# Gate features restacked by transfers, and four steps moved, in the first attention of a two-layer gated cross-attention kernel

## What is computed

```python
# queries x (layer norm), keys and values ctx; 16 batches, 128 tokens, H = 16 heads of 64
delta_x = log(clip(abs((cx - cx.T) / w), 0.001))      # delta_y alike; delta_w = log(w / w.T), delta_h alike
mul = (100.0 * stack[delta_x, delta_y, delta_w, delta_h])[..., None] * [1, 1000 ** -0.5]
emb = concatenate([sin(mul), cos(mul)])                # 16 gate features of a query-key pair
g = relu(einsum('bnmd,hd->bhnm', emb, Wg) + bg)        # one gate per head and pair
a = q @ k.T / sqrt(64)
mn = softmax(log(clip(g, 1e-6)) + a)                   # = clip(g) * exp(a), normed
x = x + tanh(g_xattn[0]) * ((mn @ v) @ Wo.T + bo)
```

## Time and profile before

| | us |
|---|---|
| median of 3 runs | 1169.16 |
| lowest and highest | 1166.68, 1172.12 |
| the profiled execution, its own time | 1164.61 |
| its span, first to last instruction | 1162.8 |

### The profile page before, as it was taken

The page is one execution under the profiler, slowest core; times in us unless marked ns, Lnnn a source line. Parts: engine busy times, 40 slices in busy tenths (PEclk is TensorE's granted clock), DMA queues, the critical chain, the costliest instruction groups (busy, mean ns, idle before and its releaser), DMA issues.

```text
span 1162.8 us, 32870 instructions
## 1 busy us (share of the span) xinstructions
PE 955.3 (82%) x12178; PEld 779.8 (67%) x12178; DVE 836.2 (72%) x1947; ACT 689.7 (59%) x1338; POOL 718.9 (62%) x811
## 2 busy tenths in 40 slices
PE   0448988899999996387878559995599999999996
PEld 0336766667777764364554248873599999999995
DVE  3997888877887775657776779985566666666663
ACT  2456878888888884145425548884354545454542
POOL 2988778886677752115341539984566766666663
PEclk9888999999999997669999869995799999999998
DMA  9276667678776756330001000000555215841251
GB/s 277 72 192 142 122 129 146 150 167 183 140 149 154 154 105 148 98 130 1 1 14 41 19 2 16 26 21 19 201 142 140 32 32 140 246 142 32 32 144 16
DMA packets 52118, 119.65 MB, mean 103 GB/s; under 512 B 7617, under 2 KB 30145, under 8 KB 51633
## 3 DMA queue, kind: packets, MB, share of 16 engines
q0 software_dynamic: 14144, 35.48, 21.3%
q1 hardware_dynamic: 35520, 80.71, 20.7%
q10 hardware_dynamic: 2352, 2.10, 0.6%
HBM read 212.54 MB, written 37.85 MB: 215 GB/s over the span
## 4 chain that ended last, share of the span: by engine, by line
PE 51%; DVE 18%; POOL 14%; ACT 6%; issue 5%; DMA 4%; POOLq 0%; ACTq 0%; SPq 0%; DVEq 0%
PE bank L2107 17%; PE bank L2121 9%; POOL PT L560 6%; PE bank L1786 6%; PE bank L1689 3%; PE bank L1766 2%; DVE nmx L1177 2%; ACT EX L1393 2%; PE bank L1728 2%; DVE h L1063 2%; PE bank L1937 2%; PE bank L1721 1%; DVE PT L923 1%; PE bank L1780 1%; DMA gates<-in_g_ffn 1%
## 5 line engine op out<-in xcount | busy, mean ns | idle before, releaser
L1623 ACT ACTIVATE yg<-bank,bms 128x128 f32<-128x128 f32 x312 | 107.8, 364 | 106.8 <-PE bank L2107 98.9
L1296 DVE TENSOR_TENSOR hm<-hf,hm 128x256 f16<-128x256 f32 x156 | 70.3, 450 | 81.5 <-ACT hm L1630 81.5
L1291 DVE SCALAR_TENSOR_TENSOR hf<-bank,bms,yg 128x128 f32<-128x128 f32 x312 | 98.1, 345 | 33.2 <-ACT yg L1623 32.0
L2107 PE MATMUL bank<-xT,wm_even 128*128 128x128 f16 x1920 | 115.6, 221 | 1.0 <-DVE xT L1303 1.0
L2107 PEld LDWEIGHTS bank<-xT,wm_even 128*128 128x128 f16 x1920 | 111.5, 99 | 2.1 <-DVE xT L1303 1.4
L560 POOL TENSOR_TENSOR PT<-PT 128x512 f16<-128x512 f32 x64 | 72.7, 1183 | 61.4 <-ACT PT L1419 61.4
L707 POOL DMA_INDIRECT out_x<-ys,sidx x39 | 62.8, 1611 | 76.2 <-DVE ys L1310 76.2
L2107 PE MATMUL bank<-xT,wm_odd 128*128 128x128 f16 x1824 | 108.0, 219 | 1.8 <-DMA wm_odd<-expert_weights 1.8
L2107 PEld LDWEIGHTS bank<-xT,wm_odd 128*128 128x128 f16 x1824 | 104.2, 98 | 2.4 <-issue 1.9
L1630 ACT ACTIVATE hm<-hf 128x256 f16<-128x256 f32 x156 | 64.5, 414 | 63.1 <-DVE hf L1291 61.7
L619 POOL TENSOR_TENSOR h<-h 128x512 f16<-128x512 f32 x32 | 40.6, 1281 | 83.0 <-DVE h L1063 81.0
(11 more groups left out here) (308 smaller groups left out, 2646.7 us busy)
## 6 DMA issues: line engine op xcount, KB each, us to landing
wm_even<-expert_weights SPq DMA_DIRECT2D x60, 1024.0 KB
wm_odd<-expert_weights SPq DMA_DIRECT2D x57, 1024.0 KB
expert_weights<-in_wcat POOLq DMA_DIRECT2D x16, 768.0 KB, 7.8
wsp<-expert_weights SPq DMA_DIRECT2D x16, 768.0 KB, 4.4
wsp<-in_wcat POOLq DMA_DIRECT2D x16, 768.0 KB, 10.3
expert_weights<-wsp SPq DMA_DIRECT2D x16, 768.0 KB, 3.3
Lst<-gate_tables SPq DMA_DIRECT2D x48, 68.0 KB, 6.0
gate_tables<-Lw SPq DMA_DIRECT2D x6, 512.0 KB, 3.3
```

The costliest lines, as they stand in the source:

```text
L1291: v.scalar_tensor_tensor(hf[:, (c // 2) % 2, c % 2, :], bank[c % 4][:, MT:2 * MT], bms[:, par, FC + c:FC + c + 1], yg[:, c % 4, :], ALU.ad ...
L1296: v.tensor_tensor(hm16[:, par, 1, c - 1:c + 1, :], hf[:, q % 2, :, :], hm16[:, par, 0, c - 1:c + 1, :], ALU.subtract).then_inc(m_hl, 1)
L1623: s.activation(yg[:, c % 4, :], bank[c % 4][:, 0:MT], ACT.Gelu, bias=bms[:, par, c:c + 1]).then_inc(m_g, 1)
L2107: ins = t.matmul(bank[c % 4][:, w * MT:(w + 1) * MT], wm16[par][:, wp, col:col + P], xT16[:, par, xp * KD + kk, :], start=(n == 0), stop=( ...
```

## The change

- **Features stacked.** The 128 feature partitions are ordered in four groups of 32 (each of 4 queries). SyncE copies them into a new tile `Fst`: for each group the high half twice and the low half once, 96 partitions. That is twelve transfers of 64 KB per batch (`stack_high`, eight; `stack_low`, four). The weight shrinks to 96 x 64, its middle 32 rows being the low half, and a query group takes four matmuls of 64 columns in place of three of 256. F16s has one buffer in place of two. The gates wait for the stacked tile.
- **Sine moved.** `feature_sine` of batch b stands behind `probs_high` of b - 1 in iteration b, in place of the end of iteration b - 1. The three negated parts of an expert half are spread before, between and behind the exponentials.
- **Value low halves** go from GpSimd (`split_v`) to VectorE (`value_low`, behind the turns).
- **Output bias.** It is scaled by the gate once and added to X by GpSimd (`out_bias`). `residual` is one operation, behind the products.
- **GpSimd's order.** `probs_low` stands ahead of `half_low`. `pv` waits for each low probability by itself. SyncE's loop holds the stacking between the tables and the expert halves; its first transfers of box data come as two of 128 rows in place of four broadcasts to 64.

```diff
+QN = 4
+QR = 2 * QN * 4
+FR = 3 * QR
+STK = 16 * 3 * (NN // QN)
...
-        F16s = sb("F16s", [P, 2, 2, NJ * N], F16, l0)
+        F16s = sb("F16s", [P, 2, NJ * N], F16, l0)
+        Fst = sb("Fst", [P, NN // QN, NJ * N], F16, l0)
...
-            for xy in range(2):
-                for e in range(2):
-                    sp.dma_start((cm, rows)[e][64 * xy:64 * xy + 64, :], a["boxm"][xy, e, :].partition_broadcast(64)).then_inc(s_cw, 16)
+            for e in range(2):
+                sp.dma_start((cm, rows)[e][:, :], a["boxm"][e]).then_inc(s_cw, 16)
...
+            def stack_high(b):
+
+                sp.wait_ge(s_fhi, b + 1)
+                if b:
+                    sp.wait_ge(s_gf, 4 * b)
+                for q in range(NN // QN):
+                    for k in range(2):
+                        sp.dma_start(Fst[k * QR:k * QR + QR, q, :], F16s[q * QR:q * QR + QR, 0, :]).then_inc(s_fst, 16)
+
+            def stack_low(b):
+
+                sp.wait_ge(s_flo, b + 1)
+                for q in range(NN // QN):
+                    sp.dma_start(Fst[2 * QR:3 * QR, q, :], F16s[q * QR:q * QR + QR, 1, :]).then_inc(s_fst, 16)
...
-            for i in range(1, B // 2 - 1):
-                for par in range(2):
-                    next_ctx(i * 2 + par, par)
-                    if i * 2 + par == NJ:
-                        store_tables(1)
-                    load_tables(i * 2 + par)
-                    store_half(i - 1, par)
-                    load_half(i, par)
-            for par in range(2):
-                load_tables(B - 2 + par)
-                store_half(E - 2, par)
-                load_half(E - 1, par)
-
+            for b in range(2, B):
+                par = b % 2
+                if b < B - 2:
+                    next_ctx(b, par)
+                if b == NJ:
+                    store_tables(1)
+                load_tables(b)
+                stack_high(b - 1)
+                stack_low(b - 1)
+                store_half(b // 2 - 1, par)
+                load_half(b // 2, par)
+
+            stack_high(B - 1)
+            stack_low(B - 1)
...
-            def split_v(b, par):
-                for r in range(2):
-                    gp.wait_ge(s_vh, 2 * b + r + 1)
-                    nc.gpsimd.tensor_tensor(vv16[:, par, 1, 8 * r:8 * r + 8, 0:DK], vf[:, r, :, :], vv16[:, par, 0, 8 * r:8 * r + 8, 0:DK], ALU.subtract).then_inc(s_vl, 1)
-
             def feature_low(n, par):
                 gp.wait_ge(s_fhi, n + 1)
-                nc.gpsimd.tensor_tensor(F16s[:, par, 1, :], fs, F16s[:, par, 0, :], ALU.subtract).then_inc(s_flo, 1)
+                if n:
+                    gp.wait_ge(s_fst, STK * n)
+                nc.gpsimd.tensor_tensor(F16s[:, 1, :], fs, F16s[:, 0, :], ALU.subtract).then_inc(s_flo, 1)
+
+            def out_bias(c):
+
+                gp.wait_ge(s_tg, 2)
+                gp.wait_ge(s_xn, c + 1)
+                return nc.gpsimd.tensor_tensor(X[:, c, :], X[:, c, :], bo[:, :], ALU.add)
...
-            split_v(0, 0)
...
                 if c:
+                    probs_low(b - 1)
                     half_low(b - 1)
-                    probs_low(b - 1)
+                    out_bias(b - 1)
                     feature_low(b, par)
                 if has_q:
                     split_qk(b + 1, 1 - par)
                 if has_x:
                     half_high(b + 2)
-                if has_q:
-                    split_v(b + 1, 1 - par)
                 if has_x:
                     split_ctx(b + 2, par)
                 if has_s:
@@ -605,8 +628,9 @@
                 iteration(b, b % 2, 2, True, True, b < NJ - 1)
             iteration(B - 2, 0, 2, True, False)
...
+            probs_low(B - 1)
             half_low(B - 1)
-            probs_low(B - 1)
+            out_bias(B - 1).then_inc(s_flo, 1)
...
-            step(v.tensor_copy(We16[:, 0, :], We[:, :]))
-            step(v.tensor_tensor(We16[:, 1, :], We[:, :], We16[:, 0, :], ALU.subtract))
+            step(v.tensor_copy(We16[0:FR, :], We[0:FR, :]))
+            step(v.tensor_tensor(We16[QR:2 * QR, :], We[QR:2 * QR, :], We16[QR:2 * QR, :], ALU.subtract))
...
-                v.tensor_tensor(otmp[:, :], bank[7][:, 0:D], bo[:, :], ALU.add).then_inc(s_opt, 1)
-                dv.wait_ge(s_opt, c + 1)
+                dv.wait_ge(s_flo, min(c + 2, B + 1))
                 xb = X[:, bass.ds(c, 1), :]
-                v.scalar_tensor_tensor(xb, otmp[:, :].unsqueeze(1), tg[:, 0:1], xb, ALU.mult, ALU.add).then_inc(s_xu, 1)
+                v.scalar_tensor_tensor(xb, bank[7][:, 0:D].unsqueeze(1), tg[:, 0:1], xb, ALU.mult, ALU.add).then_inc(s_xu, 1)
+
+            def value_low(b):
+                for r in range(2):
+                    dv.wait_ge(s_vh, 2 * b + r + 1)
+                    v.tensor_tensor(vv16[:, b % 2, 1, 8 * r:8 * r + 8, 0:DK], vf[:, r, :, :], vv16[:, b % 2, 0, 8 * r:8 * r + 8, 0:DK],
+                                    ALU.subtract).then_inc(s_vl, 1)
...
-            take_v(0, True)
+            take_v(0, (0, 1), True)
             feature_distance(1, 1)
+            value_low(0)
             dv.wait_ge(s_tg, 1)
+            v.tensor_scalar(bo[:, :], bo[:, :], tg[:, 0:1], None, ALU.mult).then_inc(s_tg, 1)
...
                     feature_floor(b + 1, 1 - par)
-                    take_v(b + 1)
+                    take_v(b + 1, (0, 1))
                     feature_turns(b + 1, 1 - par)
+                    value_low(b + 1)
                 if has_x:
                     xn_low(b + 2, par)
-                if has_c:
-                    residual(b - 1)
-                    dv.wait_ge(s_xu, b)
                 if has_q:
                     feature_fractions(b + 1, 1 - par)
                 if not has_q:
@@ -1009,6 +1038,8 @@
                     feature_distance(b + 2, par)
                 probs(b, not has_c)
                 if has_c:
+                    residual(b - 1)
+                    dv.wait_ge(s_xu, b)
                     v.bn_stats(bst[:, bass.ds(b - 1, 1), :].rearrange("p o c -> p (o c)"), X[:, bass.ds(b - 1, 1), :].rearrange("p o d -> p (o d)"))
 
             iteration(0, 0, False, True, True)
@@ -1019,7 +1050,7 @@
             iteration(B - 2, 0, True, True, False)
             iteration(B - 1, 1, True, False, False)
             ternary_hidden()
-            take_pv(B - 1)
+            take_pv(B - 1, range(4))
             residual(B - 1)
...
-                if first > 1:
-                    ac.wait_ge(s_gf, 4 * n - 4)
-                s.activation(F16s[:, par, 0, :], fs, ACT.Copy).then_inc(s_fhi, 1)
+                if n:
+                    ac.wait_ge(s_fst, STK * n)
+                s.activation(F16s[:, 0, :], fs, ACT.Copy).then_inc(s_fhi, 1)
...
-                half_negated(b, par, range(NSP - 1))
+                half_negated(b, par, (0,))
                 for g in range(4):
                     if g == 2:
-                        half_negated(b, par, (NSP - 1,))
+                        half_negated(b, par, (1,))
                     ac.wait_ge(s_st, 4 * b + g + 1)
                     if g == 0 and not first:
                         ac.wait_ge(s_pm, 8 * b)
                     s.activation(EX[:, HS * g:HS * g + HS, :], bank[g % 2][:, :].rearrange("p (h n) -> p h n", h=HS), ACT.Exp,
                                  scale=DK ** -0.5).then_inc(s_exp, 1)
+                half_negated(b, par, (2,))
...
                 if c:
                     probs_high(b - 1, c == 1)
+                    feature_sine(b, par, c)
...
                 exps(b, par, c == 0)
-                if has_q:
-                    feature_sine(b + 1, 1 - par, min(c + 1, 2))
...
-                    pe.wait_ge(s_flo, b + 1)
+                    pe.wait_ge(s_fst, STK * (b + 1))
...
-                    for n, (wp, fp) in enumerate(PAIRS):
-                        ins = t.matmul(bk[:, jj * 256:(jj + 1) * 256], F16s[:, par, fp, j * N:(j + 1) * N], We16[:, wp, :], start=False,
-                                       stop=(n == 2), skip_group_check=True)
+                    part = bk[:, jj * 256:(jj + 1) * 256].rearrange("p (h q i) -> p q h i", h=H, q=NN // QN)
+                    for q in range(NN // QN):
+                        ins = t.matmul(part[:, q, :, :], Fst[0:FR, q, j * N:(j + 1) * N], We16[0:FR, :], start=False, stop=True,
+                                       skip_group_check=True)
...
-            def pv(c, par, first):
-                pe.wait_ge(s_pl, 4 * c + 4)
+            def pv(c, par, first, fs_):
                 pe.wait_ge(s_vl, 2 * c + 2)
-                for f in range(4):
+                for f in fs_:
+                    pe.wait_ge(s_pl, 4 * c + f + 1)
                     if f == 0:
                         pe.wait_ge(s_xh, xl_of(c))
                         pe.wait_ge(s_xl, xl_of(c))
                     elif f == 1:
                         if not first:
-                            pe.wait_ge(s_opt, c)
+                            pe.wait_ge(s_xu, c)
...
```

(8 more changed lines are left out.)

53 lines of the change are left out of this document (29 added, 24 removed).

## The result

| | median, us | runs | profiled run: time, span |
|---|---|---|---|
| before | 1169.65 | 1166.68 to 1172.12 | 1164.6, 1162.8 |
| after | 1268.12 | 1264.03 to 1274.33 | 1274.3, 1272.1 |

The ratio is 1.085 (95% interval 1.080 to 1.090): 98 us slower, where +14 was forecast and 1205 us was the upper end of the range. The direction was right, the size was not.

What follows compares the result with a forecast made beforehand. VectorE's and ScalarE's chains, arriving together, were taken to bound the first attention's iteration. +0.7 - 3 + 6.3 + 10 = +14 on 1164.6 gave 1178.6, the median 1183 us; bounds 1174 to 1193, eight in ten 1168 to 1205.

Steps and rivals of the forecast that it cites:

- Part 5: Low half sent behind the low probabilities: free in the loop; at its end FFN weights come late, +10 us.
- -3 + 6.3: Loop terms at 24.3 us an iteration: -3 us for iterations 2 to 6, +6.3 us for 7 to 14.
- Rival D: VectorE stalls against GpSimd in the new overlap, or a cooler clock in longer waits: above 1190 us, chance 0.06.
- rival A: The stack is the bound: each gate waits 1.5 us for its last piece, fifteen times, +22, 1205 us, chance 0.20.
- B: Rival: at the loop's end the FFN weights come in time, tail gains 1.5 us, 1172 us, chance 0.12.
- C: Rival: VectorE's late chain was the bound and ScalarE keeps up, iterations 22.4 us, 1157 us, chance 0.07.
- Part 1: Residual behind the products, bias on GpSimd: cost 0, gain 1.6 us in a long iteration, 0 in a short one.
- Part 2: Sine moved behind the high probabilities on ScalarE: new iteration 24.3 us, of either kind.
- the train of ScalarE: ScalarE's queue from T, the products' end, to the O copies without a wait: T + 12.88 instead of T + 12.17.
- Part 3: Value low halves on VectorE: fit its 2.14 us wait in the loop; the start together +0.7 us.
- Part 4: Stacked features: TensorE's gate work 1.2 us instead of 3.3, worth 0 on the path; twelve transfers, cost 0.
- The margin of 1.2 us: Slack of the stack: pieces there at T + 16.5, T being the products' end, first gate due at T + 17.7.

Runs made afterwards that it cites:

- e5: The kernel before with GpSimd issuing the low half behind the low probabilities, in the loop and behind it: 1260.2 us, ratio 1.081.
- e4: The changed kernel with GpSimd's low half issued ahead of the low probabilities again, in the loop and behind it: 1223.5 us, ratio 1.047.
- e8: The kernel before with only the residual and its statistics moved behind the products and the bias added by GpSimd: 1176.5 us, ratio 1.009.
- e2: The kernel before with only the sine and its copy moved behind the high probabilities: 1187.2 us, ratio 1.014.
- e7: The changed kernel without the feature stack and with the low half issued ahead of the low probabilities again: 1176.2 us, ratio 1.010.
- e16: The kernel before with only the value low halves moved from GpSimd to VectorE: 1161.9 us, ratio 0.997.
- e3: The changed kernel without the stack, the gate reading its features by three pairs again: 1270.3 us, ratio 1.087.
- e12: The changed kernel with the low half issued ahead of the low probabilities and the sine back at the end of the iteration before: 1186.2 us, ratio 1.014.
- e9: e5 with one wait added, GpSimd waiting for ScalarE's absolute value between the low half's issue and the low features: 1209.1 us, ratio 1.031.
- e15: The kernel before with O copies ahead of the logarithm, norm and statistics behind the third query take, FFN loads ahead of the last store: 1159.8 us, ratio 0.995.
- e10: The kernel before with the absolute value at the end of ScalarE's iteration, the floor among the query takes, the residual behind the distances: 1184.8 us, ratio 1.011.

## Why the prediction was wrong, step by step

**Part 5 holds the step that failed**, one sentence of it: "In the loop nobody waits for it." The sum gave the loop -3 + 6.3 and the measured loop is 83.7 us longer. (8 x 24.3 - 188.3 is 6.1, not 6.3; nothing hangs on it.) Of the transfer the sentence is true. But I weighed a moved issue only by who waits for its data, and not by what it does to the engine that issues it. Moved from ahead of a wait to the middle of GpSimd's run, it makes the rest of the run block VectorE's floor. e5 gives this step alone +96 us, of which 84 between the first T and that of batch 14. The other half of part 5, the tail, came out within 0.6 us: +9.4 measured for +10 (e5, without the stack, has +8.3), VectorE idle 20.4 us ahead of the ternary reduction, and the store at 544.48, T + 16.3. It was not the only reason, though: with the half early, e4's last iteration still takes 33.3 us, because the last stack's twelve issues hold SyncE's queue until T + 13.7. The prediction had the last of them out by T + 10.6 and didn't put the stack into the tail.

**Rival D** named the collision, with its row, but not what brings it about; it gave no price beyond "above 1190", a chance of 0.06 and no place. Priced by its row, 3.3 us of stall in each of 14 iterations, it would have been +46 us. I took the 4.05 us for a chance event of the start; it was the only iteration of the kernel before in which the issue stood where the change puts it.

Rivals A, B and C did not come true in the changed kernel: TensorE waited for the stack once, 1.6 us; the halves landed in 11.1 us and the FFN weights were waited for; no iteration was shorter.

**Part 1, cost 0:** e8 measured +12. Two errors are in its trace. "GpSimd pays about 0.7 us for the bias" was taken to cost nothing: in the short iterations these 0.7 us shift the low queries so that the floor waits for one, and the O copies end 0.7 us later. And in the iterations with tables the norm takes 1.28 us, the row maxima come late, and these lead to the fourth query copy, which is ahead of the O copies in ScalarE's queue (in iteration 2 the floor starts at T + 11.2, the O copies end at T + 14.5 instead of 11.6); "they have to end before ScalarE reaches the O copies" does not hold there. The gain of 1.6 us in the long iterations didn't come; GpSimd's work stretched what was put there.

**Part 2, 24.3 us of either kind:** the train of ScalarE was right to 0.4 us in e2 (O copies at T + 13.27, forecast 12.88); the floor's 0.9 us more are the difference. In iterations with tables e2 has 26.0, and 26.8 where the projection takes 5.41 us; its residual is still ahead of the products there. With parts 1 to 3 together (e7) the iterations take 25.0 and 25.2. The three parts sum to +4 in the forecast and to +12 in e7, of which 5.3 lie between the first T and that of batch 14.

**Part 3:** right. Small, and in e16 a gain of 3 us.

**Part 4, cost 0:** true of the changed kernel (e3 is no faster without the stack), for the wrong reason. SyncE needs 0.59 us an issue, not the 0.42 of the table loads, and with what lies between them 7.9 us for twelve, so that the last goes out by T + 13.6 instead of T + 10.6; and the pieces land in 6.6 us at the median, where 6.0 was taken. The margin of 1.2 us was not there; the late iterations covered it. What rival A feared, waits for the stack, is what e4 measures. The gate's work itself is as forecast, eight matmuls of 64 columns in 0.41 us, and worth nothing: in e12 TensorE's gates are short and the iteration is set by the exponentials.

**The clock** was part of rival D too. From 320 to 498 us of the changed kernel and in one projection of the slow kind (start and end, us, busy us by engine, granted clock, DMA share, GB/s):

```profile
320.00:498.00 178.00, 141.53 (x1807) 113.28 (x1804) 134.53 (x268) 121.06 (x174) 86.08 (x78) 0.90 0.69 148
368.00:373.30 5.30, 5.30 (x19) 4.26 (x20) 4.85 (x12) 3.09 (x5) 0.00 (x0) 0.68 1.01 233
```

In the kernel before the granted clock is 1.00 from 272 to 434 us. Here it is 0.90: stretches at 1.2 instead of 2.4 GHz, in iterations in which TensorE waits 2.35 us for row maxima and 2.42 for the O copies. Where one falls on the output's projection this takes 5.41 instead of 3.72 us, the difference between the iterations of 28.4 and 30.1. In e2, e7 and e12, whose iterations are 24 to 25 us, the clock of the short iterations is 1.00 again and the projection takes 3.72. So the low clock comes with the stall and makes it dearer, by 1.7 us in the iterations that it falls on here and by 2.5 in those of e5. No run separates the two.

## What to carry to other kernels

Cost a moved transfer issue twice: by who waits for the data, and by what its own engine does right behind it. On GpSimd, put an issue where a wait follows; in the run of tensor operations behind an issue a VectorE operation of 0.7 us took 3 to 10 us here, and a wait added behind the issue was a gain of 50 to 58 us. And when one row of a profile is five times its kind, find out what is different around it before calling it a chance event: it may be the only sample of the state that the change makes the rule.

## What the runs showed of the hardware that I had not expected

- The stall behind an issue: floor 0.73 us in the kernel before, 5.3 in e5, 2.0 with a 1.2 us pause of GpSimd behind the issue (e9), 0.84 and 1.25 with chance waits of 0.41 and 0.19 us (e12, e8, iteration 0), the norm 7.7 once in e15. Operations of VectorE that read a PSUM bank (query takes, O takes) stand in the same runs at their usual 0.69 and 0.42 us; floor, turns, norm, the first of the fractions (3.3 instead of 0.7 us in e8) and, less, the residual are the ones held.
- Behind such an issue GpSimd's operations are recorded 0.4 us longer, each starting before the one ahead ends: bias 1.15 against 0.72, low features 2.54 against 2.13. After the high half's issue in e10 the stall comes without that mark.
- SyncE took 0.59 us for the issue of a 64 KB transfer within SBUF, 0.42 for a 68 KB one from DRAM; the stacked pieces landed in 6.6 us at the median (2.0 to 8.4).
